# A two-layer recurrent and attention kernel: where the experts' tanh and the copy of the turned probabilities stand in ScalarE's order

## The chip, the core and the metric

The kernel runs on one core of a Trainium2 chip. The metric is the device time of one execution in microseconds. Three executions of the kernel before took 491.16, 493.17 and 494.71 us; the median is 493.17 us.

## The reference, cut to what matters

The input `x` is 16 sequences of 256 rows of 128 features. Both layers add a gated branch to a residual:

```
layer 0:  xn = layernorm(x);  s = decaying complex recurrence(xn)   # an FFT convolution in the reference
          f  = 32 experts (top 4, silu) + shared expert (silu), times routing weights
          x  = x + s * silu(f)
layer 1:  xn = layernorm(x)
          q, k, v = xn wq' + bq, xn wk' + bk, xn wv' + bv
          s  = softmax(q k' / sqrt(128)) v                           # within one sequence
          h  = gelu(xn w_fc')            # 8 experts x 64 hidden, exact gelu, every row
          f  = sum over experts of gate_e * (h_e w_proj_e')          # top 2 of 8 gates
          x  = x + s * silu(f)
```

Everything is float32.

## The kernel before

Each engine has one program, and they meet at semaphores only. Layer 0 takes the first 317 us or so of the profile: routing, the shared expert, the recurrence, an indirect scatter of rows to expert slots, the 48 steps of the expert products, and a gather. Its last part and the norm of layer 1 are computed in pieces (pairs of sequences) that are spread into layer 1.

Layer 1 is a loop of 16 **rounds**, b = 0 to 15, one sequence each. Each engine carries out its list in the written order, so an instruction that waits holds up all that stands behind it on the same engine. All but the last two pieces of a round lie within it; the experts' sum, tanh and last product of sequence b are done in round b + 1.

**TensorE**, in order:
- the query and key products (L847) and the value product (L854);
- the scores (L861). They go to PSUM bank 6, which also holds the previous round's attention output, so they wait for that output to have been weighed (semaphore `d_os`), and for ScalarE's copy of the queries and keys;
- the hidden products of the 8 experts (L867), which wait for the gelu of the round before;
- now and then the turn of the gates (L833, rounds 0, 4, 8, 10, 12, 14) and of normalized rows (L760, rounds 0, 4, 6, 9, 11);
- the experts' sum of the round before (L825);
- **the turn** of the probabilities (L883), into bank 2;
- the gates spread over the hidden rows (L888);
- probabilities times values (L894), which waits for ScalarE's copy of the turned probabilities.

**ScalarE**, in order: the copy of queries and keys with bias (L1076), the copy of values (L1084), the exponentials (L1087), in gate rounds a copy of turned gates (L1095), the gelu of the hidden products (L1101, all 128x1024 in one instruction), the copy of the turned probabilities (L1104), and the tanh that stands for half of the silu of the round before (L1068, in `tanh_moe`). Behind these come in some rounds a small tanh for gates (L1036), a tanh for layer 0's rest (L1062), and the copies of turned rows (L1001, L1002, and L1005 in the next round). Where a function is not in ScalarE's loaded table, the trace shows an ACT_TABLE_LOAD at that function's line; it is put into the program when the kernel is built, ahead of the instruction and of that instruction's waits.

**VectorE**, in order: the row maximum of the scores (L1470) and its scaled negative (L1471), then in some rounds gates, statistics and the weighted sum of gathered expert rows (L1336), the reciprocal of the row sums (L1483), then
- in most rounds first **the product** of gelu and spread gates (L1487, in `gate_hidden`, which waits for the gelu and for L888), the finish of the round before (L1458, L1461, L1464), and then the weighing of the attention output (L1496, in `weigh_output`);
- in rounds 3, 5, 8 and 10, where `turned(b)` is not None, the weighing first and then the product and the finish.

Behind that, rounds 3, 5, 8 and 10 normalize rows (L1384), and rounds 2, 4, 7 and 9 mix layer 0's rest into `x` (L1357 to L1362).

**SyncE** loads the next sequence's turned rows and stores finished ones. **GpSimdE** gathers expert rows by indirect DMA until about 400 us.

Of the kernel before, what the change touches and what calls it, by code (L numbers as in the profile page):

```python
# [78 lines left out]
def turned(b):  # L79

    return NORM_AT.get(b)
# [10 lines left out]
def gated(b):  # L94


    if b == -1:
        return 0
    for k, (first, count) in enumerate(BATCHES[1:], 1):
        if turned(b - 2) == first + count - 1:  # L100
            return k
    return None


def batch_of(b):

    for k, (first, count) in enumerate(BATCHES):
        if first <= b // 2 < first + count:
            return k, b - 2 * first
# [16 lines left out]
def build(nc, x, phazor, phazor_init, last_re, last_im, router_w, w_gate, w_up, w_down, sh_gate, sh_up,  # L126
# [10 lines left out]
    with ctx:  # L137
# [3 lines left out]
        def sem(name):  # L141
            return ctx.enter_context(nc.semaphore(name))
# [125 lines left out]
        pT = hs_t[1]  # L268
# [7 lines left out]
        def bank(n, width=512):  # L276
            return ps[:, n, 0:width]
# [78 lines left out]
        d_pT = sem("d_pT")  # L356
        d_pTs = sem("d_pTs")
# [225 lines left out]
        def _(pe):  # L583
# [126 lines left out]
            def ids(at):  # L710

                _, v = nc.values_load_multi_w_load_instructions(
                    tile_expert[0:1, bass.ds(at, GT)], engines=[mybir.EngineType.PE], min_val=0, max_val=E0 - 1,
                    skip_runtime_bounds_check_because="VectorE clamps the ids to E0 - 1")
                return v
# [185 lines left out]
        def _(sc):  # L901
            a = nc.scalar
# [95 lines left out]
            def copy_xn(p):  # L998

                sc.wait_ge(c_xnT, p + 1)  # L1000
                a.copy(xn1T_pair, bank(7))  # L1001
                a.copy(xn_tok[:, bass.ds(p * 4, 4), :].rearrange("p a d -> p (a d)"), bank(7)).then_inc(c_xn_kept, 1)  # L1002

            def copy_gate_logits(p):
                a.copy(lg1[:, bass.ds(p * 4, 4), :].rearrange("p a e -> p (a e)"),  # L1005
                       ps[:, 7, 2 * SEQ - 4 * E1:2 * SEQ]).then_inc(c_lgs, 1)
# [27 lines left out]
            def tanh_gates(k):  # L1034
                sc.wait_ge(d_gd, k + 1)
                a.activation(gth[:], gd[:], ACT.Tanh, scale=0.5).then_inc(d_gth, 1)  # L1036
# [23 lines left out]
            def tanh_f(p):  # L1060
                sc.wait_ge(c_f, 2 * p + 2)
                a.activation(f_act, f_sb, ACT.Tanh, scale=0.5).then_inc(c_fact, 1)  # L1062

            def tanh_moe(b, first):
                sc.wait_ge(d_moe, b + 1)
                if not first:
                    sc.wait_ge(d_fin, b)
                a.activation(mth[:], bank(3, SEQ), ACT.Tanh, scale=0.5).then_inc(d_mth, 1)  # L1068

            for b in range(NSEQ):  # L1070
                u = b % 2
                sc.wait_ge(d_qk, b + 1)
                if b:
                    sc.wait_ge(d_s, b)
                for j in range(2):
                    last = a.activation(qk_sb[:, j, :], ps[:, 2, j * SEQ:(j + 1) * SEQ], ACT.Identity,  # L1076
                                        bias=bqk[:, j:j + 1])
                last.then_inc(d_qks, 1)
                sc.wait_ge(d_v, b + 1)
                if b:  # L1080
                    sc.wait_ge(d_o, b)
                if turned(b - 2) is not None:
                    copy_gate_logits(turned(b - 2))
                a.copy(v_sb, ps[:, 7, 0:SEQ].rearrange("p (a d) -> p a d", a=2)).then_inc(d_vs, 1)  # L1084
                sc.wait_ge(d_nmx, b + 1)
                for j in range(2):
                    last = a.activation(pr[:, j, :], ps[:, 6, j * SEQ:(j + 1) * SEQ], ACT.Exp,  # L1087
                                        bias=nmx[:, j:j + 1], scale=SCALE, accum_out=den[:, j:j + 1])
                last.then_inc(d_p, 1)
                batch, place = batch_of(b)  # L1090
                if place == 0:

                    sc.wait_ge(d_gT, batch + 1)
                    n = BATCHES[batch][1]
                    a.copy(gT[batch % 2][:, 0:n * 2 * SEQ],  # L1095
                           ps[0:3 * E1, 0:n, :].rearrange("p a n -> p (a n)")).then_inc(d_gTs, 1)
                sc.wait_ge(d_h, b + 1)

                if b >= 2:
                    sc.wait_ge(d_moe, b - 1)  # L1100
                a.activation(hg[u], ps[:, 4:6, :].rearrange("p a (b n) -> p (a b) n", b=2),  # L1101
                             ACT.Gelu).then_inc(d_hg, 1)
                sc.wait_ge(d_pT, b + 1)
                a.copy(pT[:].rearrange("p a b -> p (a b)"), bank(2)).then_inc(d_pTs, 1)  # L1104
                if b:
                    tanh_moe(b - 1, b == 1)
                if gated(b) is not None:
                    tanh_gates(gated(b))
                if turned(b + 1) is not None:
                    tanh_f(turned(b + 1))  # L1110
                if turned(b - 1) is not None:
                    copy_xn(turned(b - 1))
# [428 lines left out]
```

## Time and profile before

| what | value |
|---|---|
| median of three executions | 493.17 us |
| profiled execution: its own time | 494.52 us |
| its span on the core | 492.8 us |
| mean granted TensorE clock | 0.941 |
| PE busy | 389.2 us, 79% |
| DVE busy | 339.6 us, 69% |
| POOL busy | 289.1 us, 59% |
| ACT busy | 259.9 us, 53% |
| start of the first scores in layer 1 (round 0) | 321.46 us |
| start of the scores of round 15 | 476.85 us |

The profiled execution's time is 1.7 us longer than its span; the difference lies around the first and last recorded instruction. A granted clock of 1 is 2.4 GHz on TensorE and 0.5 is 1.2 GHz. From one start of the scores to the next is one round of layer 1; fifteen of them take 155.4 us.

### The profile page before, as it was taken

To read this page: it belongs to the slowest core of one execution; us is meant where nothing else is said; L and a number is where in the kernel's file an instruction comes from. 1 tells how busy PE (TensorE), PEld (TensorE's weight loads), DVE (VectorE), ACT (ScalarE), POOL (GpSimd) and SP (SyncE) were. 2 spreads that over 40 slices of the span, in tenths; PEclk is the share of its full clock that TensorE was granted. 3 is DMA by queue.
4 is the path that set the end of the run, shared out by engine and by line. 5 is a ranking of instruction groups with operands and counts; after the bars stand their busy time and mean duration, and the time that the engine had idled before them with its cause. 6 is when DMAs were issued, how large, how long until landed. Compare 5 with 4: busy or idle time off the path is not lost.

```text
span 492.8 us, 8778 instructions
## 1 busy us (share of the span) xinstructions
PE 389.2 (79%) x2516; PEld 343.8 (70%) x2516; DVE 339.6 (69%) x1166; ACT 259.9 (53%) x495; POOL 289.1 (59%) x336
## 2 busy tenths in 40 slices
PE   0717988672199999995899999869788897898895
PEld 0705777561189888884799998748677686777774
DVE  6999788989246566550138777855898989884643
ACT  1222224310156666652566775565758677678672
POOL 4995777777778777753777777067777750000000
PEclk9999998995579999996999999997999999999998
DMA  7899991111336656535467666222223220100100
GB/s 195 290 349 264 341 345 55 49 49 53 125 120 196 203 177 199 198 140 170 134 186 221 203 206 205 95 65 56 81 75 87 75 65 22 44 22 23 32 23 22
DMA packets 48205, 67.25 MB, mean 136 GB/s; under 512 B 8841, under 2 KB 25634, under 8 KB 48162
## 3 DMA queue, kind: packets, MB, share of 16 engines
q1 hardware_dynamic: 39970, 49.93, 31.4%
q0 software_dynamic: 8192, 16.79, 11.6%
q8 instruction: 22, 0.36, 0.3%
q14 instruction: 21, 0.17, 0.1%
HBM read 28.93 MB, written 35.65 MB: 131 GB/s over the span
## 4 chain that ended last, share of the span: by engine, by line
PE 30%; DVE 27%; POOL 13%; issue 10%; ACT 9%; DMA 8%; SPq 1%; DVEq 0%; ACTq 0%; POOLq 0%
POOL slot_rows L563 13%; PE ps L748 9%; DMA rows<-slot_rows 7%; PE ps L739 5%; PE ps L723 4%; DVE trig L1336 3%; PE ps L731 3%; ACT L1101 2%; PE ps L861 2%; DVE mx L1470 2%; ACT sg L973 2%; DVE rows L1487 1%; PE ps L894 1%; PE ps L847 1%; DVE act L1320 1%
## 5 line engine op out<-in xcount | busy, mean ns | idle before, releaser
L563 POOL DMA_INDIRECT slot_rows<-xn_tok,slot_of x128 | 134.3, 1049 | 43.4 <-issue 38.7
L577 POOL DMA_INDIRECT onehot<-expert_rows,slot_of x64 | 61.4, 959 | 43.0 <-DMA expert_rows<-zeros 24.1
L1320 DVE TENSOR_TENSOR act<-sg,ps 128x384 f32<-128x384 f32 x48 | 26.6, 554 | 86.2 <-ACT sg L973 85.6
L577 POOL DMA_INDIRECT route_tmp<-expert_rows,slot_of x64 | 61.8, 965 | 19.5 <-issue 19.5
L739 PE MATMUL ps<-w_dn,actT 96*128 x384 | 50.9, 276 | 1.5 <-ACT actT L991 1.5
L739 PEld LDWEIGHTS ps<-w_dn,actT 96*128 96x128 f32 x384 | 46.9, 192 | 2.0 <-issue 2.0
L723 PE MATMUL ps<-ident,rows 128*128 128x128 f32 x192 | 32.5, 296 | 15.4 <-DMA rows<-slot_rows 13.3
L973 ACT ACTIVATE sg<-ps 128x384 f32<-128x384 f32 x48 | 23.5, 490 | 38.7 <-PE ps L748 38.7
L723 PEld LDWEIGHTS ps<-ident,rows 128*128 128x128 f32 x192 | 24.1, 150 | 22.4 <-DMA rows<-slot_rows 18.4
L748 PE MATMUL ps<-w_gu,raw_fc 128*128 x192 | 37.9, 344 | 0.0
L982 ACT COPY zeros<-ps 128x512 f32<-128x512 f32 x48 | 28.1, 586 | 15.8 <-PE ps L739 15.2
L748 PE MATMUL ps<-w_gu,raw_pr 128*128 x192 | 35.7, 330 | 0.0
L825 PE MATMUL ps<-prT,rows 128*128 128x128 f32 x256 | 33.1, 285 | 1.2 <-DVE raw_fc L1464 1.2
L825 PEld LDWEIGHTS ps<-prT,rows 128*128 128x128 f32 x256 | 31.8, 199 | 2.1 <-issue 1.3
L748 PEld LDWEIGHTS ps<-w_gu,raw_fc 128*128 128x128 f32 x192 | 33.0, 203 | 0.0
L731 PE MATMUL ps<-ident,act 128*96 128x128 f32 x192 | 30.8, 284 | 2.0 <-DVE act L1320 2.0
L1487 DVE TENSOR_TENSOR rows<-rows,ps 128x1024 f32<-128x1024 f32 x16 | 19.5, 1218 | 18.5 <-PE ps L888 9.8
L867 PE MATMUL ps<-hs_t,fcT 128*128 128x256 f32 x128 | 31.0, 386 | 0.0
L748 PEld LDWEIGHTS ps<-w_gu,raw_pr 128*128 128x128 f32 x192 | 30.8, 192 | 0.0
L991 ACT COPY actT<-ps 96x512 f32<-96x512 f32 x48 | 28.0, 583 | 3.1 <-PE ps L731 3.0
L894 PE MATMUL ps<-decay_t,hs_t 128*128 128x128 f32 x128 | 18.5, 288 | 13.5 <-ACT hs_t L1104 13.4
L894 PEld LDWEIGHTS ps<-decay_t,hs_t 128*128 128x128 f32 x128 | 15.5, 191 | 18.0 <-ACT hs_t L1104 18.0
(227 smaller groups left out, 896.9 us busy)
## 6 DMA issues: line engine op xcount, KB each, us to landing
slot_rows<-zeros SPq DMA_DIRECT2D x12, 1024.0 KB, 12.7
rows<-slot_rows SPq DMA_DIRECT2D x48, 256.0 KB
expert_rows<-zeros SPq DMA_DIRECT2D x48, 256.0 KB
x_tok<-in_L_attn_x_dram SPq DMA_DIRECT2D x8, 256.0 KB, 4.9
slot_rows<-xn_tok,slot_of POOLq DMA_INDIRECT x128
hs_t<-xn_tok SPq DMA_DIRECT2D x16, 128.0 KB
out_dram<-raw_fc SPq DMA_DIRECT2D x16, 128.0 KB, 1.8
w_dn<-in_L_ffn_w_down_dram SPq DMA_DIRECT2D x1, 1536.0 KB
```

The lines of the kernel that those rows point to most:

```text
L563: g.indirect_dma_start(out=slot_rows[r], out_offset=bass.IndirectOffsetOnAxis(ap=slot_of[:, n:n + 1], axis=0), in_=xn_tok[:, r * HT + t, : ...
L577: g.indirect_dma_start(out=gath[b % 4][:, j, :], out_offset=None, in_=expert_rows[r], in_offset=bass.IndirectOffsetOnAxis(ap=slot_of[:, n: ...
L723: mm = pe.transpose(ps[:, 0, j * P:(j + 1) * P], rows[slot][:, j * P:(j + 1) * P], ident[:])
L731: mm = pe.transpose(ps[0:I0, 5, j * P:(j + 1) * P], act[u][:, j, :], ident[:])
L739: mm = pe.matmul(ps[:, 6, j * P:(j + 1) * P], actT[u][:, j * P:(j + 1) * P], w_dn[:, bass.ds(e[j] * P, P)], start=True, stop=True)
L748: mm = pe.matmul(ps[:, 1 + 2 * u + j // 2, (j % 2) * 256:(j % 2) * 256 + 2 * I0], exT[u][:, j * P:(j + 1) * P], w_gu[:, bass.ds(e[j], 1), ...
L825: mm = pe.matmul(ps[:, 3, j * P:(j + 1) * P], hg[u][:, c, j * P:(j + 1) * P], prT[:, c, :], start=(c == 0), stop=(c == CH1 - 1))
L867: mm = pe.matmul(ps[:, 4 + c // 2, (c % 2) * SEQ:(c % 2 + 1) * SEQ], fcT[:, c, :], xn1T[u], start=True, stop=True)
L894: mm = pe.matmul(ps[:, 6, j * P:(j + 1) * P], pT[:, k, j * P:(j + 1) * P], v_sb[:, k, :], start=(k == 0), stop=(k == 1))
L973: a.activation(sg[u][:].rearrange("p (a b) i -> p a b i", a=2), ps[:, 1 + 2 * u:3 + 2 * u, :].rearrange("p a (b i) -> p a b i", b=2)[:, :, ...
L982: a.copy(eo[slot], bank(6)).then_inc(e_out, 1)
L1320: v.tensor_tensor(act[u][:].rearrange("p (a b) i -> p a b i", a=2), sg[u][:].rearrange("p (a b) i -> p a b i", a=2), ps[:, 1 + 2 * u:3 + 2 ...
```

## The change

In ScalarE's list for a round, the gelu used to come first, then the copy of the turned probabilities, then the experts' tanh of the round before. Now the tanh comes first (in every round but the first, where there is none), then the copy, then the gelu. Nothing is added or removed in the source, and no other engine's list is touched.

```diff
--- before.py
+++ after.py
@@ -1094,16 +1094,16 @@
                     n = BATCHES[batch][1]
                     a.copy(gT[batch % 2][:, 0:n * 2 * SEQ],
                            ps[0:3 * E1, 0:n, :].rearrange("p a n -> p (a n)")).then_inc(d_gTs, 1)
+                if b:
+                    tanh_moe(b - 1, b == 1)
+                sc.wait_ge(d_pT, b + 1)
+                a.copy(pT[:].rearrange("p a b -> p (a b)"), bank(2)).then_inc(d_pTs, 1)
                 sc.wait_ge(d_h, b + 1)
 
                 if b >= 2:
                     sc.wait_ge(d_moe, b - 1)
                 a.activation(hg[u], ps[:, 4:6, :].rearrange("p a (b n) -> p (a b) n", b=2),
                              ACT.Gelu).then_inc(d_hg, 1)
-                sc.wait_ge(d_pT, b + 1)
-                a.copy(pT[:].rearrange("p a b -> p (a b)"), bank(2)).then_inc(d_pTs, 1)
-                if b:
-                    tanh_moe(b - 1, b == 1)
                 if gated(b) is not None:
                     tanh_gates(gated(b))
                 if turned(b + 1) is not None:
```

## Rows read from the trace of the kernel before

**Rows 1.** The page, the chain that ended last, by engine.

```profile
PE 30%; DVE 27%; POOL 13%; issue 10%; ACT 9%; DMA 8%; SPq 1%; DVEq 0%; ACTq 0%; POOLq 0%
```

**Rows 2.** Groups by line, 317 to 494 us: count, busy us, mean ns, idle before.

```profile
L1087 ACT ACT_TABLE_LOAD x16 | 20.5, 1283 | 0.3
...
L1101 ACT ACT_TABLE_LOAD x16 | 20.5, 1283 | 0.3
...
L1101 ACT ACTIVATE rows<-ps 128x1024 f32<-128x1024 f32 x16 | 16.4, 1023 | 0.2
...
L1068 ACT ACTIVATE mth<-ps 128x256 f32<-128x256 f32 x16 | 6.4, 401 | 5.7 <-PE ps L825 5.7
...
L1487 DVE TENSOR_TENSOR rows<-rows,ps 128x1024 f32<-128x1024 f32 x16 | 19.5, 1218 | 18.5 <-PE ps L888 9.8 <-ACT rows L1101 8.6
```

**Rows 3.** Timeline of round 13: start us, duration us, engine, line, idle before.

```profile
458.31 1.13 PE L861 MATMUL ps<-hs_h 128*128 128x256 f32 x4 [0.49 <-ACT hs_h L1076]
...
461.22 0.20 ACT L1087 ACTIVATION_READ_ACCUMULATOR hs_h<-ps,nmx 128x1 f32 x1
...
461.44 1.28 ACT L1101 ACT_TABLE_LOAD   x1
...
462.74 1.02 ACT L1101 ACTIVATE rows<-ps 128x1024 f32<-128x1024 f32 x1
...
462.78 0.60 PE L883 MATMUL ps<-ident,hs_h 128*128 128x128 f32 x4
...
463.66 0.58 ACT L1104 COPY hs_t<-ps 128x512 f32<-128x512 f32 x1
...
464.01 1.22 DVE L1487 TENSOR_TENSOR rows<-rows,ps 128x1024 f32<-128x1024 f32 x1 [1.66 <-PE ps L888]
...
464.29 1.16 PE L894 MATMUL ps<-decay_t,hs_t 128*128 128x128 f32 x8 [0.37 <-ACT hs_t L1104]
...
466.40 0.60 DVE L1496 SCALAR_TENSOR_TENSOR o_sb<-ps,rden,bv_all 128x128 f32<-128x128 f32 x2
...
467.24 1.13 PE L861 MATMUL ps<-hs_h 128*128 128x256 f32 x4 [0.48 <-ACT hs_h L1076]
```

**Rows 4.** Timeline, rounds 1, 6, 7 and 12: the turn, then the product.

```profile
341.47 0.60 PE L883 MATMUL ps<-ident,hs_h 128*128 128x128 f32 x4
...
343.27 1.22 DVE L1487 TENSOR_TENSOR rows<-rows,ps 128x1024 f32<-128x1024 f32 x1
...
391.87 0.60 PE L883 MATMUL ps<-ident,hs_h 128*128 128x128 f32 x4
...
394.91 1.22 DVE L1487 TENSOR_TENSOR rows<-rows,ps 128x1024 f32<-128x1024 f32 x1
...
402.50 0.60 PE L883 MATMUL ps<-ident,hs_h 128*128 128x128 f32 x4
...
403.86 1.22 DVE L1487 TENSOR_TENSOR rows<-rows,ps 128x1024 f32<-128x1024 f32 x1
...
453.69 0.60 PE L883 MATMUL ps<-ident,hs_h 128*128 128x128 f32 x4
...
454.95 1.22 DVE L1487 TENSOR_TENSOR rows<-rows,ps 128x1024 f32<-128x1024 f32 x1 [2.76 <-PE ps L888]
```

**Rows 5.** Timeline of round 3, a round with turned rows.

```profile
360.96 0.60 PE L883 MATMUL ps<-ident,hs_h 128*128 128x128 f32 x4
...
365.31 1.21 DVE L1487 TENSOR_TENSOR rows<-rows,ps 128x1024 f32<-128x1024 f32 x1
```

**Rows 6.** Timeline: TensorE after its wait in round 0, and its last sums.

```profile
330.57 1.16 PE L894 MATMUL ps<-decay_t,hs_t 128*128 128x128 f32 x8 [2.21 <-ACT hs_t L1104]
...
485.18 3.50 PE L825 MATMUL ps<-prT,rows 128*128 128x128 f32 x16 [1.19 <-DVE raw_fc L1464]
```

**Rows 7.** Stretches: busy us by engine, then granted clock, DMA share, GB/s.

```profile
330.00:336.00 6.00, 5.43 (x26) 5.04 (x27) 1.83 (x3) 2.55 (x8) 4.48 (x5) 0.65 0.22 57
336.00:341.00 5.00, 5.00 (x24) 4.34 (x23) 3.33 (x30) 4.08 (x8) 3.78 (x5) 0.73 0.21 56
```

## The prediction

> **What bounds the kernel now.** I read the page's chain first [rows 1]: TensorE, VectorE and GpSimdE share it, ScalarE has 9%, so no engine's total decides and the question is what waits for what inside a round. Then ScalarE's and VectorE's groups in layer 1 [rows 2]. ScalarE changes its table twice per round, 16 loads of 1283 ns at the exponentials and 16 at the gelu, none at the tanh. And before its product of gelu and gates VectorE idles 18.5 us in 16 rounds, 9.8 of them ended by TensorE's spread gates and 8.6 by the gelu.
>
> Then round 13 in order of time [rows 3], which rounds 12, 14 and 15 repeat. The exponentials end at 461.42. The gelu's table load starts at 461.44: it runs while TensorE is still busy with the experts' sum. The gelu follows at 462.74, the copy of the turned probabilities at 463.66, although the turn was over at 462.78 + 0.60 = 463.38. The copy releases L894 at 464.29; that, the next queries and their copy lead to the scores at 467.24. Beside this, VectorE starts the product at 464.01 and ends the weighing at 466.40 + 0.60 = 467.00. So two paths reach the next scores nearly together: one by way of the copy, and one by way of the gelu and VectorE, which has only 0.24 us left, 0.10 with the way to TensorE.
>
> **What is moved, step by step.**
>
> *The copy, earlier.* The tanh needs the experts' sum, which ends before the turn does; with 0.40 us [rows 2] it is over by about the turn's end. The copy can then start 0.04 behind the turn, at 463.42 instead of 463.66: 0.24 us gained on the path by way of the copy, up to 2.2 in round 0, where L894 waited 2.21 us for it [rows 6].
>
> *The tanh, earlier.* Nobody is late for it: its reader is the finish (L1458), behind the product. Worth nothing.
>
> *The gelu, later.* Its load no longer runs beside the sum. Tanh and copy wait for the sum and the turn, and with the tanh drawing on the table that the exponentials left, the load stands directly ahead of the gelu, behind the copy. From the start of the turn: 0.60 turn, 0.04, 0.60 copy (0.58 with its end), 1.30 load to gelu, 1.02 gelu, 0.13 to VectorE (the last small terms are gaps between rows of that round and its like; durations [rows 3]). Sum: 3.69 us. In round 13 the gelu is at VectorE at 462.78 + 3.69 = 466.47, and the product started at 464.01: 2.46 late.
>
> *Who waits.* On VectorE the finish and then the weighing stand behind the product, and TensorE's next scores wait for the weighing. From product to weighing is 466.40 - 464.01 = 2.39, then 0.60, and 0.14 to TensorE: the scores come at 466.47 + 3.13 = 469.60 instead of 467.24, 2.36 later. The gain of 0.24 is on a path that now has over 2 us of slack. No DMA hangs on this: the loads of rows follow the hidden products, the stores follow the finish, and both have a round's time.
>
> *All rounds.* Let D be the time from the start of the turn to that of the product. A round loses about 3.69 - D:
> - round 1: D = 1.80 [rows 4], loses 1.89; round 7: 1.36 [rows 4], 2.33. Rounds 2, 9 and 11 lie between rounds 6 and 7 in D; the same subtraction gives 1.16, 1.76 and 1.94, the last less 0.48 that its scores waited for other work: 1.46.
> - round 6: D = 3.04 [rows 4], as VectorE comes late from its other work: 0.65. Round 4 is like it, with the turn earlier by 0.6 because VectorE comes from round 3's normalization with TensorE already free: 0.92.
> - rounds 12 and 14: D = 1.26 [rows 4], 2.43, less 0.23 of slack at the scores: 2.20 each. Round 13: 2.36. Round 15: 2.46, nothing behind it hides it.
> - rounds 3, 5, 8, 10: VectorE is the bound and weighs first. D is 4.35 in round 3 [rows 5], more than 3.69: nothing. Rounds 5 and 8 the same. In round 10 the weighing comes 0.4 earlier: -0.4.
> - round 0 has no tanh and a late turn: the copy is earlier by 2.2, half of which is lost again because the copies of turned rows still stand behind the gelu: -1.2.
>
> Sum: 1.89 + 1.16 + 0.92 + 0.65 + 2.33 + 1.76 + 1.46 + 2.20 + 2.36 + 2.20 + 2.46 - 0.4 - 1.2 = 17.8 us.
>
> *TensorE's clock.* In rounds 1, 2, 7, 12, 13 and 14 TensorE is through with all other work about 3 us before the next scores can start: in round 13 it was through at 467.24 - 0.48 = 466.76 [rows 3], will be 0.24 earlier, and the scores come at 469.60. After its wait of 2.21 us in round 0 [rows 6] the granted clock was 0.65 over 330 to 336 and 0.73 over 336 to 341 [rows 7]: at the 1.2 GHz level for 4.2 + 2.7 = 6.9 us. A wait of 1.19 near the end was followed by sums that took 3.50 us for 16 matmuls [rows 6], where four of that shape took 0.60 in the turn [rows 3]. So I expect the clock to fall in those rounds and to give a slow scores-to-turn stretch, which is on the path now. Below: nothing; above: 6.9 us at half speed, 3.4 us a round. I take half a slow stretch of that size, 1.5 us, in rounds 2, 13, 14 and 15, and 0.5 to 0.8 in rounds 3, 5, 7, 10 and 12, where the wait is shorter or VectorE has slack: 6 + 3 = 9 us.
>
> Total +26.8, less 1 more for round 0, where the wait that lowered the clock is gone and part of round 1 may run at full clock: **+25.8**. The profiled execution took 494.52; 494.5 + 25.8 = 520.3. It is 1.35 above the median of 493.17, so against the median **519 us**.
>
> **A rule on the price of a load.** After the exponentials end at 461.42 the load starts at 461.44, and the gelu starts 1.30 behind it [rows 3]: a switch costs 1.30 us here, and the sum uses that. The Trainium skill (ScalarE: Activation LUTs, "What ACT_TABLE_LOAD costs") says otherwise: 1283 ns for the load and about 1380 ns of drain with each switch; by it each of the eleven exposed loads would cost 1.38 more, some 15 us above my total. The rows show no such drain.
>
> **Rivals.**
>
> *A, the clock holds.* TensorE keeps 2.4 GHz across the new waits. For it: a wait of 0.5 us each round does nothing now. Against: [rows 6, 7]. Then 494.5 + 17.8 - 1.35 = 511 us.
>
> *B, the load stays hidden.* Which tables hold exponential and tanh together no row shows, as every tanh in layer 1 runs behind a gelu. If the exponentials' table lacked it, the load would stand ahead of the tanh, hidden beside the sum, and the gelu would come 1.30 earlier: rounds 2, 4 and 6 lose nothing, the others about 1.1 in rounds 12 to 15, 1.0, 0.6, 0.5 and 0.2 in rounds 7, 1, 9 and 11: 6.3 - 1.2 = +5, 498 us. Against: a tanh never brings a load of its own [rows 2]. The Trainium skill (ScalarE: Activation LUTs, "Table sets: the hidden batching unit") lists tanh in the exponentials' set too, which speaks for my order of events.
>
> *C, faster.* The copy was what the next round waited for, and its 0.24 to 2.2 us come through. Place: L894, which waits for the copy in every round; price: 0.2 to 0.4 in rounds 12 to 14, about 1 in five others and up to 4 in rounds 0 and 1 with the clock, -8 us, 485. It decides only where the gelu reaches VectorE no later than the spread gates, and the order of rows says that it comes 2.46 later.
>
> *D, no difference.* B's load with C's gain in rounds 0 and 1 at full clock: about 493.
>
> **How the numbers follow.** Forecast 68%, A 20%, B 6%, D 3%, C 3%. The range is to hold 8 in 10: from 505, below A with 6 us for a mistake in D's subtraction, to 531, where the slow stretches cost 2.5 instead of 1.5 us. About 1% is what a measurement of this kernel can tell from no change. B's 498 lies at that bound and is shared between same and slower. Faster 0.03, same 0.06, slower 0.91.
>
> **What would show it.** Loads still 16 and 16 at the two lines; the gelu's starting right behind the copy, 0.6 us behind the turn's end; VectorE's idle time before the product up from 18.5 to some 35 us or more, now ended by the gelu; the scores released by the weighing; round 13 lasting 11.3 us at full clock, more at a lower one, instead of 8.93; rounds 3, 5 and 8 hardly longer. The mean granted clock under 0.94. The prediction is wrong if the load stands ahead of the tanh, or if VectorE weighs before its product in ordinary rounds.

## The result and the profile after

The changed kernel takes 520.86 us (median of four executions, 519.66 to 526.4), the kernel before on the same chip 492.22 (491.16 to 494.71). The ratio is 1.060, with a 95% interval of 1.054 to 1.066: slower by 29 us at the medians. The forecast was 519. The profiled executions differ by less, 519.87 against 494.52, and their spans by 518.1 - 492.8 = 25.3 us; the accounting below is made between these two. The gap of the medians is wider because the profiled execution of before is among its longest (494.52 against a median of 492.22) and that of the changed kernel is below its median.

ScalarE's groups in layer 1, from 317 us to the end, with the same columns as [rows 2]; the gelu is now at L1105. Then, from the page of the changed kernel, VectorE's product.

```profile
L1087 ACT ACT_TABLE_LOAD x16 | 20.5, 1283 | 0.3
L1105 ACT ACT_TABLE_LOAD x16 | 20.5, 1283 | 0.3
L1105 ACT ACTIVATE rows<-ps 128x1024 f32<-128x1024 f32 x16 | 16.4, 1024 | 0.2
...
L1068 ACT ACTIVATE mth<-ps 128x256 f32<-128x256 f32 x16 | 6.1, 383 | 29.2 <-PE ps L825 29.2
```

```profile
L1487 DVE TENSOR_TENSOR rows<-rows,ps 128x1024 f32<-128x1024 f32 x16 | 19.5, 1220 | 46.1 <-ACT rows L1105 46.1
```

Nothing was added: 32 loads before and after, at the same price, and none at the tanh, which in rounds 1 to 15 now runs right behind the exponentials (the sixteenth, behind the loop, follows the last gelu). What moved is idle time. ScalarE waits 29.2 us for the experts' sum ahead of the tanh, and VectorE idles 46.1 us before its product instead of 18.5, all of it ended by the gelu. TensorE, for its part, waits 21.3 us for the weighing ahead of the scores instead of 4.1; the same group in the kernel before and in the changed one:

```profile
L861 PE MATMUL ps<-hs_h 128*128 128x256 f32 x64 | 18.4, 413 | 8.1 <-DVE o_sb L1496 4.1 <-ACT hs_h L1076 4.0
L861 PE MATMUL ps<-hs_h 128*128 128x256 f32 x64 | 22.1, 478 | 23.0 <-DVE o_sb L1496 21.3 <-ACT hs_h L1076 1.4
```

The timeline of round 13 of the changed kernel answers to [rows 3].

```profile
473.09 1.22 PE L861 MATMUL ps<-hs_h 128*128 128x256 f32 x4 [3.09 <-DVE o_sb L1496]
...
474.11 3.50 PE L867 MATMUL ps<-hs_t,fcT 128*128 128x256 f32 x8
...
477.44 1.95 PE L825 MATMUL ps<-prT,rows 128*128 128x128 f32 x16
...
479.23 0.60 PE L883 MATMUL ps<-ident,hs_h 128*128 128x128 f32 x4
479.43 0.38 ACT L1068 ACTIVATE mth<-ps 128x256 f32<-128x256 f32 x1 [3.13 <-PE ps L825]
479.87 0.59 ACT L1100 COPY hs_t<-ps 128x512 f32<-128x512 f32 x1
480.47 1.28 ACT L1105 ACT_TABLE_LOAD   x1
...
480.50 1.16 PE L894 MATMUL ps<-decay_t,hs_t 128*128 128x128 f32 x8
...
481.76 1.02 ACT L1105 ACTIVATE rows<-ps 128x1024 f32<-128x1024 f32 x1
...
482.92 1.22 DVE L1487 TENSOR_TENSOR rows<-rows,ps 128x1024 f32<-128x1024 f32 x1 [5.70 <-ACT rows L1105]
...
485.30 0.60 DVE L1496 SCALAR_TENSOR_TENSOR o_sb<-ps,rden,bv_all 128x128 f32<-128x128 f32 x2
...
486.05 1.10 PE L861 MATMUL ps<-hs_h 128*128 128x256 f32 x4 [3.08 <-DVE o_sb L1496]
```

The product starts 482.92 - 479.23 = 3.69 us behind the turn, where it was 464.01 - 462.78 = 1.23 [rows 3]. The copy is 0.04 behind the turn's end and has gained its 0.2 us, but the next scores no longer ask for it: they are released by the weighing (o_sb L1496), and TensorE has waited 3.08 us. The round takes 12.96 us instead of 8.93. Of these 4.03, the longer way from turn to next scores gives 486.05 - 479.23 = 6.82 against 467.24 - 462.78 = 4.46, or 2.36. The rest, 1.67, lies between scores and turn, 6.14 against 4.47: the hidden products (L867) took 3.50 us, where those of round 14 took 1.89. The clock tells why (stretches of the changed kernel, columns as in [rows 7]):

```profile
330.00:336.00 6.00, 5.50 (x38) 5.22 (x39) 4.15 (x32) 3.86 (x10) 4.48 (x6) 1.00 0.21 57
336.00:341.00 5.00, 3.90 (x29) 3.12 (x27) 3.60 (x11) 4.41 (x9) 3.78 (x5) 1.00 0.21 53
472.00:476.00 4.00, 2.91 (x9) 2.39 (x10) 2.50 (x11) 0.94 (x4) 0.00 (x0) 0.74 0.20 66
476.00:480.00 4.00, 4.00 (x28) 3.49 (x27) 1.05 (x7) 0.82 (x4) 0.00 (x0) 0.83 0.00 0
```

Over 472 to 480, behind a wait of 3.09 us, the clock was granted at 0.74 and 0.83: at the 1.2 GHz level for 4 x 0.26 x 2 = 2.08 and 4 x 0.17 x 2 = 1.36 us, 3.4 together. The first two lines are the other side: the slow stretch of the kernel before [rows 7] is gone, since L894 no longer waits in round 0. From the first scores to the last it is 177.41 us instead of 155.39; the first start 1.02 earlier, and what follows the last scores takes 4.30 longer: 22.02 - 1.02 + 4.30 = 25.3 us.

Round 13 is not the only slow one, and a wait for the weighing is not the only wait that a slow stretch followed. From scores to turn, rounds 2, 5, 8, 10, 12, 13 and 15 take 1.6 to 1.8 us longer than before, round 7 1.0. Rounds 5, 7, 10 and 12 are those where TensorE had just waited 1.37 or 1.89 us for ScalarE's copies of turned rows (L1002), which stand behind the gelu and came late with it; the kernel before has no such wait. That these shorter waits lowered the clock is likely by the order of the rows, and no run tests it. Round 12:

```profile
457.44 1.03 PE L766 MATMUL ps<-g1T,decay 128*128 128x8 f32 x8 [1.37 <-ACT xn_tok L1002]
...
459.61 1.38 PE L861 MATMUL ps<-hs_h 128*128 128x256 f32 x4 [0.58 <-DVE o_sb L1496]
460.78 3.34 PE L867 MATMUL ps<-hs_t,fcT 128*128 128x256 f32 x8
```

L766 is a small product from the turned rows; there are five such waits, 7.9 us together. Behind the fifth, ahead of round 1, the clock held.

### The profile page after: what moved, and what is told of

Same layout as the page of the kernel before. It is cut to its first block, busy times and chain, and to the rows that moved or that the text cites. A ratio compares the mean times of both kernels' runs of the same rounds, so it can differ in the third digit from the quotient of the medians.

```text
span 518.1 us, 8778 instructions
## 1 busy us (share of the span) xinstructions
PE 400.8 (77%) x2516; PEld 350.0 (68%) x2516; DVE 338.5 (65%) x1166; ACT 261.8 (51%) x495; POOL 290.2 (56%) x336
## 4 chain that ended last, share of the span: by engine, by line
PE 40%; DVE 17%; POOL 13%; issue 11%; ACT 11%; DMA 7%; SPq 1%; DVEq 0%; ACTq 0%; POOLq 0%
POOL slot_rows L563 13%; PE ps L748 9%; DMA rows<-slot_rows 6%; PE ps L867 6%; PE ps L825 5%; PE ps L739 5%; PE ps L861 4%; PE ps L723 4%; ACT L1105 3%; ACT rows L1105 2%; PE ps L731 2%; ACT sg L973 2%; PE ps L883 1%; DVE mg L1461 1%; DVE o_sb L1496 1%
## 5 line engine op out<-in xcount | busy, mean ns | idle before, releaser
L1487 DVE TENSOR_TENSOR rows<-rows,ps 128x1024 f32<-128x1024 f32 x16 | 19.5, 1220 | 46.1 <-ACT rows L1105 46.1
L861 PE MATMUL ps<-hs_h 128*128 128x256 f32 x64 | 22.1, 478 | 23.0 <-DVE o_sb L1496 21.3
L867 PE MATMUL ps<-hs_t,fcT 128*128 128x256 f32 x128 | 38.5, 455 | 0.0
L867 PEld LDWEIGHTS ps<-hs_t,fcT 128*128 128x128 f32 x128 | 30.9, 241 | 6.2
L1087 ACT ACTIVATE hs_h<-ps,nmx 128x256 f32<-128x256 f32 x32 | 14.9, 470 | 35.6 <-DVE nmx L1471 35.6
L861 PEld LDWEIGHTS ps<-hs_h 128*128 128x128 f32 x64 | 12.8, 223 | 27.0 <-issue 21.0
```

The source lines that it names most:

```text
L861: mm = pe.matmul(ps[:, 6, j * SEQ:(j + 1) * SEQ], qk_sb[:, 0, j * P:(j + 1) * P], qk_sb[:, 1, :], start=True, stop=True)
L867: mm = pe.matmul(ps[:, 4 + c // 2, (c % 2) * SEQ:(c % 2 + 1) * SEQ], fcT[:, c, :], xn1T[u], start=True, stop=True)
```

## The experiments

Each kernel is timed beside the kernel before on its chip, and compared by that ratio. The first four (early_load, copy_only, tanh_only and kept_clock) ran on a chip where the program was held up in layer 0 by waits of up to 87 us (the kernel before took 737.12 us there), so that only their differences in us and their last rounds can be read; all four, kept_clock with half as many added matmuls, were run again on other chips, with _2 behind the name. A timeline shows one execution, which can lie some us beside the median of its kernel.

**The load put back under the sum (early_load, early_load_2).** In the changed kernel, ahead of the tanh (the line that makes the tile `early` is left out here):

```diff
+                a.activation(early[:, b:b + 1], iota_p[:], ACT.Gelu)
```

> The changed kernel, with one gelu of 128x1 put behind the exponentials of every round (its result is not used), so that the gelu's table is loaded there, beside TensorE's sum, and tanh and copy follow with that table. My theory (the load standing between copy and gelu delays the product): the product follows the start of the turn by 2.4 us instead of 3.69, round 13 takes about 10.0 us at full clock, the whole 498 to 502 us. Rival (the loss comes from the gelu standing behind the copy at all, or from TensorE's clock alone, and the load costs nothing): 515 us or more.

On the stretched chip: 748.78 us against 737.12, +11.7. Then:

> The same kernel as early_load once more, where layer 0 is not stretched by long waits. My theory, corrected by what the first run's rounds showed (10.4 to 10.8 us each for rounds 8 to 14, so some slow clock remains): 500 to 505 us. Rival (the load costs nothing): 515 us or more.

Measured: 498.17 us against 492.70, ratio 1.010 (1.007 to 1.014), just under the 500 to 505 of this expectation and inside the 498 to 502 of the first. The profiled execution was its longest, 504.46 us, but 4.05 us of that come ahead of layer 1: its first scores start at 325.51 instead of 321.46. From there it takes 5.9 us longer than the kernel before, close to the 5.5 between the medians. The timeline of its round 13 (L884 is the turn, L1098 the added gelu, L1489 the product):

```profile
465.38 1.10 PE L862 MATMUL ps<-hs_h 128*128 128x256 f32 x4 [1.67 <-DVE o_sb L1498]
...
468.49 1.28 ACT L1098 ACT_TABLE_LOAD   x1
469.78 0.20 ACT L1098 ACTIVATE early<-iota_p 128x1 f32<-128x1 f32 x1
469.83 0.60 PE L884 MATMUL ps<-ident,hs_h 128*128 128x128 f32 x4
470.47 0.59 ACT L1102 COPY hs_t<-ps 128x512 f32<-128x512 f32 x1
470.95 1.03 ACT L1107 ACTIVATE rows<-ps 128x1024 f32<-128x1024 f32 x1
...
472.11 1.22 DVE L1489 TENSOR_TENSOR rows<-rows,ps 128x1024 f32<-128x1024 f32 x1 [2.71 <-ACT rows L1107]
...
475.25 1.10 PE L862 MATMUL ps<-hs_h 128*128 128x256 f32 x4 [1.67 <-DVE o_sb L1498]
```

The load is done before the turn starts; the product is 2.28 us behind the turn, the round 9.87 us (9.86 in the run on the stretched chip). One instruction of 0.20 us takes back some five sixths of the loss: the 1.41 us by which the product comes earlier, and, since TensorE now waits 1.67 us and keeps its clock (1.00 over 456 to 485), the slow stretches with them: in no round is the way from scores to turn over 5.7 us, where the changed kernel has seven rounds above 6.1. The rival, a load that costs nothing, is out.

**Half of the change: only the copy ahead (copy_only, copy_only_2).** The tanh stays behind the gelu.

> Half of the change: only the copy of the turned probabilities goes ahead of the gelu, the tanh stays behind it. My theory (the gelu and its load wait for the turn because the copy does): as the changed kernel, 517 to 523 us, the product again about 3.7 us behind the start of the turn. Rival (the tanh ahead, which waits for the experts' sum, does the harm): about 493 us.

On the stretched chip: +32.8 us (769.93). Again elsewhere:

> The same kernel as copy_only once more: only the copy goes ahead of the gelu. My theory: as the changed kernel, 517 to 524 us. Rival (the tanh's place matters too): outside that by more than 3 us.

Measured: 522.74 against 490.75, ratio 1.068 (1.063 to 1.073). The product is again 3.69 us behind the turn in rounds 13 to 15. Half of the change gives the whole loss.

**The other half: only the tanh ahead (tanh_only, tanh_only_2).** The copy stays behind the gelu.

> The other half: only the tanh goes ahead of the gelu, the copy stays behind it. My theory: the load starts when the tanh ends, some 0.2 us behind the start of the turn plus 0.4, the product comes 3.0 us behind the start of the turn, and the copy is now about 2 us late too, so that both paths are longer: 507 to 514 us. Rival (the tanh alone is free, as I took it to be for its reader): about 493 us.

On the stretched chip: +32.0 us (769.11), outside what I had expected. Again:

> The same kernel as tanh_only once more. The first run took 32 us more than the kernel before, and I had expected 15 to 22, because I had left the slower clock out of it. With the clock in: 517 to 525 us, as much as the whole change. Rival (the tanh alone costs clearly less than the whole change): 507 to 514 us.

Measured: 530.57 against 492.70, ratio 1.071 (1.062 to 1.079), slower even than I then thought. The product comes 3.05 us behind the turn, as worked out. The load is again behind something that waits for the sum, and the copy is now behind load and gelu. TensorE's idle time in layer 1 shows where that lands:

```profile
L894 PE MATMUL ps<-decay_t,hs_t 128*128 128x128 f32 x128 | 22.8, 333 | 36.9 <-ACT hs_t L1106 36.9
L861 PE MATMUL ps<-hs_h 128*128 128x256 f32 x64 | 21.8, 472 | 3.4 <-ACT hs_h L1076 3.1
```

It waits 36.9 us for the copy, 13.4 in the kernel before. The late copy also hits rounds 3, 5, 8 and 10, where VectorE weighs first: 11.02, 13.45, 12.61 and 12.68 us, against 9.03, 10.57, 11.70 and 10.93 with the whole change. So tanh ahead and copy ahead are not two costs that add up: either puts the load behind the sum, and the copy ahead at least spares the copy.

**The clock by itself (kept_clock, kept_clock_2).** Matmuls in TensorE's wait; the first result is overwritten. The diff is that of kept_clock_2.

```diff
+                if b in (2, 3, 8, 13, 14, 15):
+                    pe.wait_ge(d_hg, b)
+                    for c in range(CH1):
+                        pe.matmul(ps[:, 4 + c // 2, (c % 2) * SEQ:(c % 2 + 1) * SEQ], fcT[:, c, :],
+                                  xn1T[u], start=True, stop=True)
```

> The changed kernel with 8 matmuls of the hidden products' shape put ahead of the scores of rounds 2, 3, 8, 13, 14 and 15 (done twice, the first result is overwritten), where TensorE waits 3.1 us for the weighing; they take 1.7 to 1.9 us of that wait. My theory (the waits lower TensorE's clock, which lengthens scores to turn): the clock of 350 us to the end rises towards 1, rounds 13 to 15 take 11.3 to 11.8 us each, the whole 510 to 514 us. Rival (the rest of the loss has nothing to do with the clock): 519 to 522 us.

kept_clock added eight matmuls, each of the four twice, and they took 3.6 us, more than the wait. On the stretched chip: +20.5 us (757.66). With the four of the diff:

> The changed kernel with the hidden products' four matmuls done once more ahead of the scores of rounds 2, 3, 8, 13, 14 and 15. In kept_clock twice as many took 3.6 us, more than the wait of 3.1 us; here they take 1.8 and leave 1.3 us of it, so that they delay nothing by themselves. My theory (waits of 3.1 us lower TensorE's clock): rounds 13 and 14 take 11.3 and 11.6 us, the clock behind round 12 is 1, the whole 509 to 514 us. Rival (the clock is not what lengthens them): 519 to 523 us.

Measured: 512.98 against 490.75, ratio 1.043 (1.038 to 1.047) where the whole change has 1.060. Its timeline from round 13's scores to round 14's (L860 are the added matmuls, L866 the scores, L888 the turn) and its clock:

```profile
472.46 1.10 PE L866 MATMUL ps<-hs_h 128*128 128x256 f32 x4 [1.22 <-DVE o_sb L1501]
...
476.91 0.60 PE L888 MATMUL ps<-ident,hs_h 128*128 128x128 f32 x4
...
480.52 1.99 PE L860 MATMUL ps<-hs_t,fcT 128*128 128x256 f32 x8
483.73 1.10 PE L866 MATMUL ps<-hs_h 128*128 128x256 f32 x4 [1.22 <-DVE o_sb L1501]
```

```profile
475.00:500.00 25.00, 22.29 (x143) 18.93 (x142) 9.20 (x26) 14.26 (x28) 0.00 (x0) 1.00 0.05 17
```

Round 13 takes 11.27 us, the turn 4.45 behind the scores, at a clock of 1.00; round 14 takes 11.80. More matmuls, and the kernel is some 8 us faster than without them (1.7% of 491; the intervals of the two ratios do not touch). That the clock has a part in the loss is shown. The 8 us are not the whole of it: of the six filled places, four had a slow stretch in the changed kernel (rounds 2, 8, 13 and 15) and have none here, 6.7 us from scores to turn in all, but rounds 7, 9 and 12, where nothing was added, take 6.14, 6.58 and 6.65 us from scores to turn.

**The weighing ahead of the product (weigh_first, weigh_first_alone).** On VectorE, in all rounds:

```diff
-                if turned(b) is not None:
-                    weigh_output()
-                    gate_hidden()
-                else:
-                    gate_hidden()
-                    weigh_output()
+                weigh_output()
+                gate_hidden()
```

With ScalarE's new order:

> The changed kernel, with VectorE weighing the attention output ahead of its product in all 16 rounds, as rounds 3, 5, 8 and 10 do already. My theory (the late gelu costs time because the weighing, and so the next scores, stand behind the product): the scores are released by the copy of queries and keys instead, which stands behind the gelu on ScalarE; an ordinary round takes about 8.9 us, the clock stays near 1, the whole 488 to 497 us. Rival (the late gelu costs by itself, through ScalarE's queue or the finish and the next sum): 505 us or more.

Measured: 500.05 against 492.70, ratio 1.014 (1.008 to 1.020). The product still comes 3.66 us behind the turn, but the rounds are near the 8.9 worked out, 9.34, 8.82 and 9.34 us for 12 to 14, and the scores are released by the copy of queries and keys:

```profile
475.08 1.02 ACT L1105 ACTIVATE rows<-ps 128x1024 f32<-128x1024 f32 x1
475.09 0.61 DVE L1496 SCALAR_TENSOR_TENSOR o_sb<-ps,rden,bv_all 128x128 f32<-128x128 f32 x2 [3.70 <-PE ps L894]
476.00 0.83 ACT L1076 ACTIVATE hs_h<-ps,bqk 128x256 f32<-128x256 f32 x2
476.20 1.22 DVE L1487 TENSOR_TENSOR rows<-rows,ps 128x1024 f32<-128x1024 f32 x1 [0.50 <-ACT rows L1105]
...
476.88 1.13 PE L861 MATMUL ps<-hs_h 128*128 128x256 f32 x4 [0.60 <-ACT hs_h L1076]
```

The total missed its range by 3 us; rounds 4 and 9 take 13.06 and 13.17 us where the kernel before has 11.45 and 11.25. The profiled execution is its shortest, 496.95 us. The control, this order of VectorE with the kernel before:

> The kernel before, ScalarE's order unchanged, with VectorE weighing the attention output ahead of its product in all rounds. It is the control of weigh_first, which took 500 us where I had expected up to 497. My theory (weighing first makes VectorE wait for TensorE in the rounds that VectorE bounds, and that is what weigh_first has lost in rounds 4 and 9): 493 to 498 us. Rival (the loss of weigh_first is all the late gelu's, through the copies of turned rows behind it): 488 to 492 us.

Measured: 500.27 against 490.75, ratio 1.023 (1.017 to 1.029), beyond both. In its layer 1 VectorE waits for the attention output ahead of the weighing:

```profile
L1496 DVE SCALAR_TENSOR_TENSOR o_sb<-ps,rden,bv_all 128x128 f32<-128x128 f32 x32 | 9.8, 347 | 37.0 <-PE ps L894 36.9
```

It was 0.9 us in the kernel before. My theory named the wrong place for the cost, though: in the control rounds 4 and 9 take 10.64 and 10.10 us, less than in the kernel before. All fifteen rounds together take 1.7 us more (157.08), and what follows the last scores takes 18.17 us instead of 15.95, 2.2 more; weigh_first has the same long end, 18.32. Why rounds 4 and 9 are long in weigh_first stays open.

Weighing first costs about 2% by itself, and with it ScalarE's new order costs nothing more (1.014 with it, 1.023 without; the intervals overlap). The same edit to ScalarE's list costs 6% or nothing, depending on what stands behind the product on VectorE.

**Trying for a faster kernel (early_and_weigh_first, then early_weigh_copies).** The early load and the weighing first together, then with the copies of turned rows ahead of the gelu as well:

> Both: the extra gelu of 128x1 behind the exponentials, and the weighing ahead of the product in all rounds, on ScalarE's new order. My theory: the copy's earlier start is no longer paid for, round 13 takes about 8.6 us instead of 8.93, the whole 484 to 491 us, faster than the kernel before. Rival (the finish behind the product delays the row maximum of the next round, or TensorE is the bound): 491 to 496 us.

Measured: 494.36 against 492.70, ratio 1.004 (1.000 to 1.007). Rounds 13 and 14 take 8.71 and 9.23 us, 0.2 and 0.4 less than in the kernel before, near the 8.6 expected; the total is not faster and lies in the rival's range. In the profile, of the shortest of ten executions (491.63 us), the rounds up to the last scores take 151.68 us instead of 155.39, and the rest of the way 18.0 instead of 15.95: the long end of the weighing-first kernels takes back part of what the rounds gain.

> early_and_weigh_first, with the copies of turned rows (L1001, L1002) ahead of the gelu too, behind the copy of the turned probabilities. My theory (in rounds 4, 6, 9 and 11 TensorE waited up to 1.9 us for these copies behind the gelu): some 1 us less in each of rounds 0, 4, 9 and 11, 488 to 492 us. Rival (those rounds are bound by VectorE): 493 to 496 us.

Measured: 494.18 against 490.75, ratio 1.006 (1.002 to 1.009). It lies in the rival's range and my theory falls: the copies ahead bring nothing that can be measured. No version beats the kernel before.

## Why the prediction was right

*The gelu, later.* Right in sign and size. Its sum of 3.69 us from turn to product is what twelve of the sixteen rounds show, 13, 14 and 15 among them, to the hundredth; early_load_2 shows that the load makes 1.41 of it.

*Who waits.* Right: the scores are released by the weighing, 2.36 us later in round 13 as worked out, and weigh_first takes this wait away.

*The copy, earlier.* It starts 0.04 behind the turn's end as said, and gains nothing in ordinary rounds. Of rival C's gains only that of rounds 0 and 1 came, 2.3 us in all, and C is out.

*The tanh, earlier: worth nothing.* True beside the copy (copy_only_2 is as slow as the whole). It would have been wrong as a statement about the tanh alone: tanh_only_2 is 7% slower. I looked only at who reads the tanh, not at what its wait holds up.

*TensorE's clock and all rounds: here luck helped.* The table splits each round's loss at the turn. "To turn" is what the way from scores to turn got longer, where a slow clock shows; "behind turn" is the rest of the round. The forecast's terms stand beside them, with 0.6 us of clock for each of rounds 3, 5, 7, 10 and 12.

| rounds | behind turn, forecast | measured | clock, forecast | to turn, measured | both, forecast | measured |
|---|---|---|---|---|---|---|
| 0, 1 | +0.7 | -0.5 | -1.0 | -1.8 | -0.3 | -2.3 |
| 2 to 5 | +2.1 | +1.2 | +2.7 | +3.5 | +4.8 | +4.7 |
| 6 to 9 | +4.7 | +3.6 | +0.6 | +2.8 | +5.3 | +6.4 |
| 10 to 12 | +3.3 | +3.4 | +1.2 | +3.6 | +4.5 | +7.0 |
| 13, 14 | +4.6 | +4.6 | +3.0 | +1.6 | +7.6 | +6.2 |
| 15 and the end | +2.5 | +2.6 | +1.5 | +1.7 | +4.0 | +4.3 |
| sum | +17.8 | +15.0 | +8.0 | +11.3 | +25.8 | +26.3 |

Two errors of some 3 us cancel. The waits were put too high: round 0 gained 2.4 where 1.2 was taken, rounds 3, 5 and 8 gained 1.7 together behind the turn where nothing was taken, and round 9 lost 0.5 less. The clock was put too low: 9 us less 1, by analogy with one slow stretch of round 0, against 11.3. Of the four rounds with 1.5 us each, 2, 13 and 15 show 1.65 to 1.68 and round 14 nothing; rounds 5, 8, 10 and 12 show 1.60 to 1.76 where 0.6 or, in round 8, nothing was taken. The forecast saw no wait for the copies of turned rows in rounds 5, 7, 10 and 12. So rounds 5 and 8, said to be hardly longer, took 1.40 and 1.03 us more. The single rounds of the clock were guesses. Measured less the 1.0 by which the first scores start earlier, it is the 25.3 us between the spans, and 519.87 for the profiled execution, where 520.3 was forecast.

*A, the clock holds.* Its 511 is not reached by kept_clock_2's 512.98, which still has three slow stretches; that the two lie close says little.

*B, the load stays hidden.* As a fact wrong, loads stayed at the gelu; as a calculation it is near what early_load_2 does, 5.5 us between the medians for a forecast of 5. By that run the order tanh, copy, gelu costs 1% and the place of the load, with the slow stretches that its waits bring, the rest.

## What to carry to other kernels

A table load is placed ahead of the first instruction that needs the table, so an edit that moves this instruction moves 1.3 us of load too: look at what wait the load was hiding under, and whether it still does. When an instruction is put ahead of another on an in-order engine, its wait is inherited by all that stand behind it; ask what the late one's reader has queued behind it, here the weighing behind the product. And count what a new wait on TensorE does to its clock: here filling six waits with matmuls gave back some 8 of 29 us, over a quarter, and by the profile the way from scores to turn, where the slow stretches lie, has 11.3 of 26.3 us.

## What the hardware showed

That exponentials and tanh draw on one table was open in the trace of before and is shown now: 15 tanhs behind exponentials with no load at L1068. A switch costs 1.30 us from the load's start to the next function's, in front of the gelu in both kernels, and the load starts 0.01 to 0.02 us behind the instruction ahead of it; no drain is seen. TensorE's clock fell behind waits of 3.1 us in some rounds (13) and not in others (14), and also in round 12 behind waits of 1.37 and 0.58 us (granted 0.59 over 459.6 to 463.6); it stayed at full level behind waits of 1.67 and 1.22 us in the last rounds of early_load_2 and kept_clock_2, and the slow stretch of round 13 lasted some 3.4 us.
